# A four-layer graph network on one core: the last three message passes in groups of eight tiles, with rows as the stationary operand and transposed sums

## The reference

```python
# layer 2: edge softmax by destination; the kernel carries the denominator as column 49
rst = segment_sum(soft_label[src] * a[:, None], dst, N)      # a = exp(e) / sum of exp(e)
x = x + elu(rst)
# layer 3: twice the same weighted sum
for _ in range(2):
    h = segment_sum(h[src] * edge_weight[:, None], dst, N)
    avg = avg + h / 3
x = x + avg
```

## Time and profile before

| what | value |
|---|---|
| three runs, median (lowest to highest) | 12,126.67 us (12,122.02 to 12,133.5) |
| the profiled execution: span from first to last instruction | 14,505.6 us |
| its own time beside the span | none is listed |
| busy share of the span: PE, PEld, DVE, ACT, POOL | 42%, 33%, 30%, 26%, 64% |
| granted TensorE clock | 1.000 throughout |
| span of the light passes in the trace (first gather to last) | 2,562, 2,564 and 2,578 us |
| DMA engines busy in a light pass | 11 to 12% |

### The profile page before, as it was taken

One profiled execution on the slowest core, in us unless ns is written; L12 is line 12 of the kernel. 1 busy time (PEld: TensorE's weight loads), 2 busy tenths in 40 slices (PEclk: granted clock), 3 DMA queues, 4 the chain that ended last, 5 costly groups with the idle time before them and its releaser, 6 DMA issues. The chain is left out here.

```text
span 14505.6 us, 217117 instructions
## 1 busy us (share of the span) xinstructions
PE 6101.2 (42%) x41742; PEld 4794.2 (33%) x41743; DVE 4404.3 (30%) x18474; ACT 3763.8 (26%) x13496; POOL 9272.0 (64%) x8348
## 2 busy tenths in 40 slices
PE   4444444444555555552333333233333333333333
PEld 2222122123444444442333333233333333333333
DVE  4444444445444444443111111211111111111111
ACT  2444444443222222221111111111111111111111
POOL 5555555555888888884666666566666666666665
DMA  4333333334455555542111111111111111111111
GB/s 115 101 102 100 97 96 95 94 96 66 62 61 61 61 61 62 61 61 47 16 16 16 16 16 16 20 16 16 16 16 16 16 22 16 16 16 16 16 16 21
DMA packets 805018, 671.16 MB, mean 46 GB/s; under 512 B 417876, under 2 KB 663828, under 8 KB 802727
## 3 DMA queue, kind: packets, MB, share of 16 engines
q0 software_dynamic: 452736, 234.14, 14.8%
q1 hardware_dynamic: 349659, 430.53, 11.3%
q10 hardware_dynamic: 2588, 6.12, 0.1%
HBM read 562.94 MB, written 107.13 MB: 46 GB/s over the span
## 5 line engine op out<-in xcount | busy, mean ns | idle before, releaser
L725 POOL DMA_INDIRECT table<-table,idx x4992 | 4900.3, 982 | 3003.1 <-issue 1544.4
L801 PE MATMUL psum_acc<-table 128*128 128x48 f32 (+1 forms) x12288 | 2854.8, 416 | 5083.8 <-DVE acc L765 2683.5
L801 PEld LDWEIGHTS psum_acc<-table 128*128 128x128 f32 x12288 | 2697.3, 329 | 5241.3 <-issue 5241.3
L1071 POOL DMA_INDIRECT sums<-rows,idx x1664 | 2620.6, 1575 | 577.2 <-issue 435.1
L504 POOL DMA_INDIRECT rows<-table,idx x1668 | 1689.8, 1013 | 1593.6 <-ACT idx L554 1109.8
L775 DVE TENSOR_TENSOR table<-iota,dstf 128x512 f32 x1536 | 1063.9, 693 | 2852.3 <-remote 1462.0
L732 ACT CAST idx<-srow 128x4 int32 (+1 forms) x1266 | 243.2, 193 | 6337.6 <-DVEq L783 4122.5
L765 DVE TENSOR_TENSOR acc<-acc,psum_acc x1539 | 311.8, 203 | 3547.7 <-remote 2403.7
L693 PE MATMUL psum_acc<-parts,onehot 128*128 128x48 bf16 x6144 | 338.4, 215 | 1633.2 <-DVE onehot L637 1504.7
L992 PE MATMUL psum_exp<-table,onet 128*128 x6144 | 431.8, 219 | 1384.6 <-DVE onet L915 1141.0
L743 ACT ACTIVATE table<-table,w 128x48 f32<-128x48 f32 x3328 | 840.9, 323 | 12.0 <-DMA table<-table,idx 12.0
(11 more groups left out here) (183 smaller groups left out, 7772.8 us busy)
## 6 DMA issues: line engine op xcount, KB each, us to landing
drow<-rows_dram SPq DMA_DIRECT2D x832, 128.0 KB
lrow<-in_logit_rows SPq DMA_DIRECT2D x416, 256.0 KB
table<-table,idx POOLq DMA_INDIRECT x4992
srcrow<-rows_dram SPq DMA_DIRECT2D x416, 128.0 KB
hid_dram<-hid SPq DMA_DIRECT2D x416, 96.0 KB
hid<-hid_dram SPq DMA_DIRECT2D x416, 96.0 KB
rows<-table,idx POOLq DMA_INDIRECT x1668
sums<-rows,idx POOLq DMA_INDIRECT x1664
```

What stands on the lines that cost most here:

```text
L725: pool.indirect_dma_start(out=ring[:, u, 0:cols], out_offset=None, in_=src_table, in_offset=bass.IndirectOffsetOnAxis(ap=idx[:, u:u + 1], ...
L801: last = nc.tensor.matmul(psum_acc[:, ds(win & 1, 1), 0:cols].rearrange("p r c -> p (r c)"), hot[:, j % 2, u, :], ring[:, j * G + u, 0:col ...
L1071: pool.indirect_dma_start(out=sums[c], out_offset=bass.IndirectOffsetOnAxis(ap=idx[:, slot:slot + 1], axis=0), in_=rows[:, slot, 0:CS], in ...
```

## The change

It replaces `light_pass` and what feeds it:

- A group is eight tiles (LT = 8), 208 groups in a pass, eight to a turn (26 turns). The ring has 64 slots and lies where `cw` and `adapt` of the second pass were.
- In place of the loop over blocks, each group takes one span of 128 nodes that begins at the group's smallest destination (`bases`, made in the setup). A loop around the pass repeats it with spans moved on by 128 as often as the widest group needs (`rounds`). A group here has 1,024 edges at 17 edges to a node on average, some 60 nodes; the padded last one spans under 128 too, so there is one round.
- DVE writes `hot` as 128 x 1024 (four buffers), and does the weighing, which ACT did, as one product over the group's eight tiles (128 x 384, or 392 in the first of the three).
- PE takes the gathered rows as the stationary operand (48 or 49 columns) and the one-hot matrix as the moving one (128 columns). The result is transposed, features on partitions and nodes along them, in four PSUM banks in turn. DVE adds it (48 x 128) two groups late to `acc_t`, at the offset that is the group's smallest node.
- ACT only stages indices, sixteen columns at a time. POOL waits for them once in two groups, and for its slots' last use (`s_picked`) in each group.
- At the end of a pass PE turns the 98 blocks back, each with one f32 matmul (`acc_t` block stationary, an identity of 48 or 49 columns moving), ten blocks to a PSUM bank, two banks in turn, and ACT copies each bank to `total`.
- The setup makes the smallest node of each group and its count of spans (small DVE operations), sends them through HBM like the ranges, and makes the identity.

The diff, cut to its core (of the removed lines of `light_pass`, only marks are left):

```diff
+LT = 8
+LW = LT * P
+NL = T // LT
+LB = 8
+LU = LB * LT
+LTURNS = NL // LB
+LAG = 2
+HOTS = 4
+COLS = NPAD + P
+BATCH = 10
...
+        arena = sb("arena", [P, NBW * CS + NBW * PARTS * CT // 2 + NB * CS + 16])
...
+        edges = sb("edges", [P, 2 * T + G])
...
+        idx_light = rows_flat[:, 0:LU].bitcast(i32)
+        moved = rows_flat[0:1, LU:LU + NL].bitcast(i32)
+        counts = rows_flat[0:1, LU + NL:LU + 2 * NL].bitcast(i32)
...
-        ring = tbl_flat[:, 0:DEPTH * G * CS].rearrange("p (s c) -> p s c", c=CS)
-        hot = tbl_flat[:, DEPTH * G * CS:DEPTH * G * CS + 2 * GW].rearrange("p (r u e) -> p r u e", r=2, u=G)
+        ring = edges[:, 0:LU * CS].rearrange("p (s c) -> p s c", c=CS)
+        hot = arena[:, 0:HOTS * LW].rearrange("p (r u e) -> p r u e", r=HOTS, u=LT)
+        acc_t = arena[0:CS, HOTS * LW:HOTS * LW + COLS]
...
-                sp.wait_ge(s_rangeout, 16)
+                for k in range(2):
+                    sp.dma_start(bases_dram[k], wk_i[0:QS, 2 * GS + k * GS // 2:2 * GS + (k + 1) * GS // 2]).then_inc(s_rangeout, 16)
+                sp.wait_ge(s_rangeout, 48)
                 sp.dma_start(ranges[0:1, :], ranges_dram.rearrange("q j -> (q j)").unsqueeze(0)).then_inc(s_rangein, 16)
-                sp.wait_ge(s_rangein, 16)
+                sp.dma_start(bases[0:1, :], bases_dram[0].rearrange("q j -> (q j)").unsqueeze(0)).then_inc(s_rangein, 16)
+                sp.dma_start(counts, bases_dram[1].rearrange("q j -> (q j)").unsqueeze(0)).then_inc(s_rangein, 16)
+                sp.wait_ge(s_rangein, 48)
...
+                first = wk_i[0:QS, 2 * GS:5 * GS // 2]
+                count = wk_i[0:QS, 5 * GS // 2:3 * GS]
+                link(nv.tensor_reduce(out=first, in_=lo.rearrange("q (j k) -> q j k", k=2), axis=X_AXIS, op=ALU.min))
+                link(nv.tensor_reduce(out=count, in_=hi.rearrange("q (j k) -> q j k", k=2), axis=X_AXIS, op=ALU.max))
+                link(nv.tensor_tensor(count, count, first, ALU.subtract))
+                link(nv.tensor_scalar(count, count, NB_BITS, None, ALU.logical_shift_right))
...
+                link(nv.tensor_scalar(ident[:, :], iota[0:CS, 0:CS], node[0:CS, 0:1], None, ALU.is_equal))
+                link(nv.tensor_reduce(out=rounds[:, :], in_=counts, axis=X_AXIS, op=ALU.max))
+                link(nv.tensor_scalar(rounds[:, :], rounds[:, :], 1.0, None, ALU.add))
...
+        picks = [psum_acc[:, 0, :], psum_acc[:, 1, :], psum_exp[0][:, :], psum_exp[1][:, :]]
+        BATCHES = -(-NB // BATCH)
...
+        def light_rounds(eng, order):
+            if order == 0:
+                eng.reg_mov(done_reg[eng], 0)
+            eng.load(rounds_reg[eng], rounds[0:1, 0:1])
+            return eng.snap(rounds_reg[eng], min_val=1, max_val=NB)
         def light_pass(order, name, src_table, cols, weights, total, before=None):
...
             s_clear = sem(name + "_clear")
...
+            column = acc_t[0:cols, :]
             with nc.Block() as block:
                 @block.gpsimd
                 def _(pool):
...
+                    times = light_rounds(pool, order)
+                    with pool.Fori(0, times):
+                        with pool.Fori(0, LTURNS):
+                            done = pool.snap(done_reg[pool])
+                            for j in range(LB):
+                                if j % 2 == 0:
+                                    pool.wait_ge(s_staged, done + (j + 2))
+                                    pool.sem_inc(s_seen, 1)
+                                pool.wait_ge(s_picked, done + (j + 1))
+                                pool.sem_inc(s_seen, 1)
+                                for u in range(j * LT, (j + 1) * LT):
+                                    pool.indirect_dma_start(
+                                        out=ring[:, u, 0:cols], out_offset=None, in_=src_table,
+                                        in_offset=bass.IndirectOffsetOnAxis(ap=idx_light[:, u:u + 1], axis=0)).then_inc(s_landed_light[j], 16)
+                            pool.reg_add(done_reg[pool], done_reg[pool], LB)
                 @block.scalar
                 def _(act):
...
+                    times = light_rounds(act, order)
+                    if order == 0:
+                        act.sem_inc(s_ready, LB)
+                    with act.Fori(0, times):
+                        with act.Fori(0, LTURNS) as i:
+                            done = act.snap(done_reg[act])
+                            for j in range(0, LB, 2):
+                                act.wait_ge(s_ready, done + (j + 2))
+                                nc.scalar.copy(idx_light[:, j * LT:(j + 2) * LT], srow[:, ds(i * LU + j * LT, 2 * LT)]).then_inc(s_staged, 2)
+                            act.reg_add(done_reg[act], done_reg[act], LB)
+                    for b in range(BATCHES):
+                        n = min(BATCH, NB - b * BATCH)
+                        act.wait_ge(s_turned, order * BATCHES + b + 1)
+                        nc.scalar.copy(total[:, b * BATCH * cols:(b * BATCH + n) * cols], psum_mlp[b % 2][:, 0:n * cols]).then_inc(s_back, 1)
                 @block.vector
                 def _(dve):
                     if before is not None:
                         before(dve)
...
+                    nv.memset(column, 0.0).then_inc(s_clear, 1)
+                    nv.tensor_copy(moved, bases[:, :]).then_inc(s_moved, 1)
+                    dve.wait_ge(s_clear, 1)
+                    times = light_rounds(dve, order)
                     if order == 0:
                         dve.sem_inc(s_kept, 1)
...
+                        dve.reg_mov(moves_reg, 0)
+                    for late in late_regs:
+                        dve.reg_mov(late, NPAD)
+                    def keep(done, j, base, s_made):
+                        room = column[:, ds(base, P)]
+                        dve.wait_ge(s_kept, done + (j + 1 + LAG * order))
+                        dve.wait_ge(s_picked, done + (j + 1 + LB - LAG))
+                        nv.tensor_tensor(room, room, picks[(j - LAG) % HOTS][0:cols, 0:P], ALU.add).then_inc(s_made, 1)
+                    with dve.Fori(0, times):
+                        dve.reg_add(moves_reg, moves_reg, 1)
+                        dve.wait_ge(s_moved, dve.snap(moves_reg))
+                        dve.sem_inc(s_seen, 1)
+                        with dve.Fori(0, LTURNS) as i:
+                            done = dve.snap(done_reg[dve])
+                            dve.load(base_regs, moved[0:1, ds(i * LB, LB)])
+                            base = [dve.snap(r, min_val=0, max_val=NPAD) for r in base_regs]
+                            late = [dve.snap(r, min_val=0, max_val=NPAD) for r in late_regs] + base
+                            for j in range(LB):
+                                nv.tensor_tensor(hot[:, j % HOTS, :, :],
+                                                 iota[:, ds(base[j], P)].unsqueeze(1).to_broadcast([P, LT, P]),
+                                                 dstf[:, ds(i * LU + j * LT, LT)].unsqueeze(2).to_broadcast([P, LT, P]),
+                                                 ALU.is_equal)
+                                dve.wait_ge(s_landed_light[j], done * (16 * LT // LB) + 16 * LT)
+                                nv.tensor_tensor(ring[:, j * LT:(j + 1) * LT, 0:cols], ring[:, j * LT:(j + 1) * LT, 0:cols],
+                                                 weights[:, ds(i * LU + j * LT, LT)].unsqueeze(2).to_broadcast([P, LT, cols]),
+                                                 ALU.mult).then_inc(s_ready, 1)
+                                keep(done, j, late[j], s_kept)
+                            for k in range(LAG):
+                                dve.reg_mov(late_regs[k], base[LB - LAG + k])
+                            dve.reg_add(done_reg[dve], done_reg[dve], LB)
+                        nv.tensor_scalar(moved, moved, float(P), float(NPAD), ALU.add, ALU.min).then_inc(s_moved, 1)
+                    dve.reg_add(moves_reg, moves_reg, 1)
+                    dve.wait_ge(s_moved, dve.snap(moves_reg))
+                    dve.sem_inc(s_seen, 1)
+                    done = dve.snap(done_reg[dve])
+                    for j in range(LAG):
+                        keep(done, j, dve.snap(late_regs[j], min_val=0, max_val=NPAD), s_kept)
                 @block.tensor
                 def _(pe):
+                    times = light_rounds(pe, order)
                     if order == 0:
...
+                        pe.sem_inc(s_picked, LB)
+                    with pe.Fori(0, times):
+                        with pe.Fori(0, LTURNS):
+                            done = pe.snap(done_reg[pe])
+                            for j in range(LB):
+                                pe.wait_ge(s_ready, done + (j + 1 + LB))
+                                for u in range(LT):
+                                    last = nc.tensor.matmul(picks[j % HOTS][0:cols, 0:P], ring[:, j * LT + u, 0:cols], hot[:, j % HOTS, u, :],
```

(70 more changed lines are left out.)

60 lines of the change are left out of this document (17 added, 43 removed).

## The result

The changed kernel takes 12,492.96 us in the median (12,486.14 to 12,497.41, four runs), the kernel before 12,126.48. The ratio is 1.0301, with a 95% interval of 1.0288 to 1.0313: 3.0% slower, where 12,570 us was forecast.

The account below looks back on a forecast made before the run. The prediction took POOL's stream of indirect DMAs, never starved, to bound the kernel. 12,127 + 307 (gathers' length) + 132 (turning back) + 5 (pass starts and ends) + 2 (setup) = 12,573, stated as 12,570 us; range 12,200 to 12,710.

Parts of the forecast that it names:

- POOL's stream bounds all five passes: In the timed kernel POOL never starves; each pass lasts its number of indirect DMAs times their price.
- Part 1: Light passes: new one-hots hold one gather per group 0.76 us, 474 us, less 167 for the old ones: +307 us.
- part 3: Pass starts and ends: register loads, grown memset beside the first gathers, last weighing; +5 us for three passes, -5 to +20.
- first rival: One-hot starts after the gather at s + 3.74, which goes free; 12,099 us, 0.2% faster; chance 0.10, mixture 0.14.
- s + 3.64: 3.64 us after the start s of a group's last gather; a one-hot beginning later holds nothing of the gather at s + 3.74.
- Part 2: Pass ends: turning back 98 blocks, 196 PE records at 0.218 us, bare; 3 x 44 = +132 us.
- Part 3 and 4: Pass starts and ends, +5 us, and the setup's four linked DVE operations and four more small DMAs, +2 us (1 to 8).
- Part 5: Work of DVE, PE and ACT in the light passes' groups, and POOL's two new waits, cost nothing beside POOL's gathers.
- The lock both ways: Rival: DVE's operations also wait for a gather's end, then each holds the next gather; 12,680 us; chance 0.07.
- The profiled span: Changed kernel's trace should shrink by some 900 us, to about 13,600, while the timed run grows.

Follow-up runs that it names:

- undisturbed profile: The kernel before, without an edit, profiled a second time (also called before again): span 12,123.4 us beside 12,125.17 us of its single run.
- 200 columns: Changed kernel with a memset of 200 columns on DVE between each group's addition and the next one-hot: 12,581.38 us.
- 800 columns: Changed kernel with a memset of 800 columns on DVE between each group's addition and the next one-hot, without a wait: 12,928.53 us.
- 600 columns and wait: Changed kernel with a memset of 600 columns after the addition and a DVE wait for its end before the next one-hot: 12,315.45 us.
- copy first: Changed kernel with the copy of the bases ahead of the memset of the transposed sums instead of behind it: 12,459.14 us.
- operand in PSUM: Changed kernel with the one-hots' first operand read from PSUM and destinations made relative to their group's smallest ahead of the passes: 12,157.16 us.
- kernel before with its cure: Kernel before with the destinations copied to PSUM once ahead of the light passes and read there by its one-hots: 11,978.13 us.
- first profile: Profile of the unchanged kernel before on which the prediction was made: its trace was 2,379 us too long against the timed runs.

## Why the prediction was right, step by step

**POOL's stream bounds all five passes.** Shown. The undisturbed profile starves nowhere, and in each run the time moves by what the gathers' length moves. Held time below is the gathers' busy time less 4992 x 0.944 = 4,712.4 us; it includes 7 to 8 us under `average`, and 35 us of the copy where that was not moved:

| kernel | held, us | against the changed kernel | measured time against it |
|---|---|---|---|
| changed | 382.0 | | |
| 200 columns | 471.3 | +89 | +88 |
| 800 columns | 815.3 | +433 | +436 |
| 600 columns and wait | 210.7 | -171 | -178 |
| copy first | 349.2 | -33 | -34 |
| operand in PSUM | 45.8 | -336 | -336 |

**Part 1, the gathers' length: +307 forecast, +225 measured.** Right in mechanism and place, mis-sized in three terms. The new one-hots hold 382.0 - 35 - 7 = 340 us for a forecast of 474, since the one-hot starts at s + 3.21 and not at 3.4 (it begins 0.20 us after the addition does, where I had 0.29 and a pause of 0.1), and in the first group of a turn at 4.36, a load that the forecast does not have; the mean hold is 340 / 624 = 0.55 us instead of 0.76. The old ones held 4869.4 - 4712.4 - 7.8 = 149 for a forecast of 167. And 35 us were not foreseen: part 3 priced the grown memset at nothing and did not look at the copy behind it; counted there, they exceed that part's own bound of +20. 340 - 149 + 35 = 226. That the sum came within 80 us is partly luck: 134 us too many for the new one-hots stand against 18 and 35 the other way.

**The point from which the first rival decides, s + 3.64, was wrong in kind.** I counted from the one-hot's start. The runs with 800 and with 600 columns show that the issue counts: a one-hot that runs 0.35 us after the gather's start held it in the one, where it was issued ahead, and did not in the other, where it was issued behind. In the changed kernel DVE has nothing to wait for between addition and one-hot in seven groups of eight, so that more work on DVE could not have let the gather through there. In the first group of a turn, behind the load, the rival came true: the gather at s + 3.75 went free, and the next met the one-hot. In the profile before, no one-hot stood in line for long, and the two accounts could not be told apart there.

**Part 2, the turning back: +132 forecast, +130 measured** (43.9 + 42.2 + 43.6 at the passes' ends). The price of the earlier trace rows was good for it because both matmuls ran at the same step of 0.213 us; at the higher clock the step is 0.11, as the last section shows. Part 3 and 4: +7 forecast, +6 measured at the two starts. The heavy passes differ by 7 us, in which the change has no part that I can name; the first heavy pass's stream was 2,210 to 2,228 us long in the various runs, 2,211 in the kernel before and 2,210 in the changed one with the copy first, so it may be scatter.

**Part 5, what costs nothing.** Right. The weighing on DVE holds next to nothing: with the one-hots cured, all that is left of 45.8 us but 3 is the copy and `average`. Fewer windows earn nothing: the pauses between the gathers are the same in both kernels, and the kernel before with 512 windows a pass and four ACT scalings a group is the fastest once its one-hots are cured.

**The lock both ways** is out: the gather at 9006.84 began inside the one-hot and was held, but the weighing began at 9005.59 together with a gather and took 0.58 us; the one-hots take 1,205 to 1,228 ns. The Trainium skill, "SBUF — State Buffer", Who interferes with whom, exempts a DVE instruction with at most one SBUF input, outside the modes that take both ports; the trace agrees, with 0.94 us for the gather begun in the one-hot that reads PSUM, and 945 ns as the mean in the kernel before with its cure. That page counts a copy among the operations that can take both ports, and the run with the copy first agrees. That page also says that the order of issue decides who blocks; the trace agrees, with 2.32 us for the gather that began 0.35 us ahead of a one-hot issued before it. That such an instruction holds while it still stands in line behind another one, for as long as that one takes, is what the runs here show.

**The profiled span** was forecast at about 13,600 and is 12,491. The error was to take the long pauses of the first profile as a property of profiling this program. They belonged to that one execution; the reason is open.

## What to carry to other kernels

Where POOL issues an indirect DMA for every tile, count its stream first (number times price, and pauses) and hold the sum against the timed runs: all other work in the loop is cover, and what is left to lose or gain is what lengthens a gather and what stands after the last one. In these runs a DVE operation with two SBUF operands held the gathers that began between its issue and its end (by the time left to its end, less 0.13 us), also while it stood in line behind a long operation that itself held nothing; a short copy of one row did the same. Put one operand in PSUM (336 us here), or let a short copy go ahead of the long operation (34 us). Work that is moved from the loop to its end becomes bare there, whatever the loop saved.

## What the runs showed of the hardware that was not expected

**The clock of the kernel before was probably not 1.000.** The trace of the changed kernel has clock records from 5,680.9 us on, and they alternate between 1.00 and 0.50, the two levels of 2.4 and 1.2 GHz, while PE is busy for some 3.6 us in every 10.6. The traces of the kernel before have no clock record at all, and a view prints 1.00 for such a stretch. Busy time and clock of each stretch, before again and changed:

```profile
5640.00:7768.00 2128.00, 976.00 (x4088) 907.58 (x4088) 453.42 (x1026) 476.20 (x2076) 1620.83 (x1664) 1.00 0.14 20
```

```profile
5653.00:7859.00 2206.00, 745.36 (x3312) 640.77 (x3312) 408.11 (x624) 20.42 (x100) 1698.52 (x1664) 0.59 0.14 19
12438.00:12481.00 43.00, 42.02 (x196) 41.89 (x196) 0.18 (x1) 5.50 (x10) 0.00 (x0) 0.50 0.00 0
```

The matmuls tell the levels apart. PE's busy time (records in brackets) and the clock in two stretches of the second turning back of the changed kernel:

```profile
10170.10:10172.60 2.50, 2.50 (x23) 1.00 0.00 0
10180.00:10182.50 2.50, 2.50 (x14) 0.50 0.00 0
```

Where the records say 1.00, one of these f32 records follows the last after 0.112 us, and where they say 0.50, after 0.213. The light passes' matmuls L864 have 0.110 and 0.213, and 0.213 too in the group that ran ahead of the first clock record. In the kernel before, L801 has a median step of 0.214 and the form of the earlier trace rows one of 0.213, and none under 0.212 (profiled again). So a stretch without a record went at the pace of the lower level, and I take it that the kernel before ran at 1.2 GHz throughout; no clock record shows it.

In the light passes the level costs nothing, since PE stands beside POOL's stream. In the turning back it does: the first and the last take 42.02 us, the second 39.48, as 25 of its records fell into a stretch at 1.00. At the higher level all 196 would take some 22 us (an estimate, from 0.112 us a step). In transpose mode the step was 0.107 us at 0.50, and 0.062 at 1.00.
